# First attention of a two-layer network on one Trainium2 core: the maxima enter the scores as two more rows of the turned queries

## The reference

```python
    def _L0_attn_ref(...):
        scale = 1.0 / np.sqrt(D)
        sin, cos = _rope_tables(n, D)
        qkv = (x @ w_qkv.T + b_qkv).reshape(b, n, 3, H, D).transpose(2, 0, 3, 1, 4)
        q, k, v = (qkv[0], qkv[1], qkv[2])
        q = jax.nn.elu(q) + 1.0
        k = jax.nn.elu(k) + 1.0
        q = _apply_rope(q, sin, cos)
        k = _apply_rope(k, sin, cos)
        attn = jnp.einsum('bhnd,bhmd->bhnm', q, k) * scale
        attn = jax.nn.softmax(attn, axis=-1)
        attn_out = jnp.einsum('bhnm,bhmd->bhnd', attn, v)
        ...
        return attn_out + lepe
```

## Time and profile before

| | us |
|---|---|
| median of 3 runs | 1029.71 |
| lowest, highest of the 3 | 1021.74, 1030.68 |
| the profiled execution | 1020.3 |
| its span in the trace | 1018.5 |
| PE busy over the span | 862.1 (85%) |
| DVE busy over the span | 749.3 (74%) |
| mean granted TensorE clock | 0.915 |

### The profile page before, as it was taken

One profiled execution on the slowest core, in us unless ns is written; L12 is line 12 of the kernel. 1 busy time (PEld: TensorE's weight loads), 2 busy tenths in 40 slices (PEclk: granted clock), 3 DMA queues, 4 the chain that ended last, 5 costly groups with the idle time before them and its releaser, 6 DMA issues.

```text
span 1018.5 us, 23321 instructions
## 1 busy us (share of the span) xinstructions
PE 862.1 (85%) x7492; PEld 655.8 (64%) x7492; DVE 749.3 (74%) x2654; ACT 520.8 (51%) x1365; POOL 284.5 (28%) x395
## 2 busy tenths in 40 slices
PE   4899989999996899945999188999999998548992
PEld 3457856667765457833999166677767776437992
DVE  7758888788767866877577658877787778566675
ACT  4233044666564223014465238877887788434653
POOL 3034035634001003117755180001000000077741
PEclk9999995999996999965899679999999999859996
DMA  9204079810006304056231256645454552343313
GB/s 238 71 1 141 1 280 374 264 52 2 2 1 161 80 1 141 1 168 187 80 84 34 84 147 194 185 123 159 149 174 139 157 155 84 92 143 90 104 36 125
DMA packets 134947, 119.74 MB, mean 118 GB/s; under 512 B 10755, under 2 KB 115227, under 8 KB 134836
## 3 DMA queue, kind: packets, MB, share of 16 engines
q1 hardware_dynamic: 130292, 109.83, 36.4%
q0 software_dynamic: 4544, 8.54, 2.5%
HBM read 67.45 MB, written 51.80 MB: 117 GB/s over the span
## 4 chain that ended last, share of the span: by engine, by line
PE 63%; DVE 16%; ACT 12%; issue 4%; DMA 3%; DVEq 1%; SPq 0%; POOL 0%; POOLq 0%; ACTq 0%
PE psum L955 7%; PE psum L964 6%; PE psum L1551 6%; PE psum L1465 5%; ACT a_L L2799 3%; ACT a_L L2797 3%; PE psum L2139 3%; PE psum L2669 3%; PE psum L2718 3%; PE psum L2077 3%; PE psum L2705 2%; PE psum L2042 2%; PE psum L743 2%; PE psum L1491 2%; ACT a_PT L2808 2%
## 5 line engine op out<-in xcount | busy, mean ns | idle before, releaser
L2297 DVE TENSOR_REDUCE a_negmax<-psum 128x2 f32<-128x512 f32 x128 | 83.7, 684 | 20.9 <-PE psum L2077 19.5
L2246 ACT ACTIVATE a_PT<-psum 128x1024 f32<-128x1024 f32 x64 | 65.5, 1023 | 26.2 <-PE psum L2122 25.8
L2799 ACT ACTIVATE a_L<-a_L,a_least 128x256 f32<-128x256 f32 x128 | 63.3, 495 | 0.0
L1010 ACT ACTIVATE f_hT<-psum,f_wt 128x128 f32<-128x128 f32 x156 | 44.5, 369 | 36.5 <-PE psum L955 36.5
L1010 ACT ACTIVATE g_hT<-psum,g_wt 128x128 f32<-128x128 f32 x156 | 44.4, 370 | 33.3 <-PE psum L955 33.3
L2669 PE MATMUL psum<-a_KT,a_Q 64*128 64x128 f32 (+1 forms) x512 | 57.6, 342 | 3.3 <-DVE a_least L2859 0.9
L2797 ACT ACTIVATE a_L<-a_L,a_least 128x128 f32<-128x128 f32 x128 | 50.6, 395 | 10.7 <-DVE a_least L2859 9.8
L2857 DVE CUSTOM_DVE_ANT_0 a_L<-psum,a_X 128x128 f32<-128x128 f32 x128 | 36.6, 286 | 25.0 <-PE psum L2669 24.9
L2116 PE MATMUL psum<-a_turned 24*128 24x256 f32 x256 | 53.8, 359 | 0.0
L2859 DVE CUSTOM_DVE_ANT_0 a_L<-psum,a_X 128x256 f32<-128x256 f32 x128 | 53.7, 420 | 0.0
L2808 ACT ACTIVATE a_PT<-psum 128x768 f32<-128x768 f32 x64 | 51.2, 800 | 1.7 <-PE psum L2685 0.9
(11 more groups left out here) (579 smaller groups left out, 2563.3 us busy)
## 6 DMA issues: line engine op xcount, KB each, us to landing
z<-a_G SPq DMA_DIRECT2D x32, 512.0 KB, 3.5
a_X<-z SPq DMA_DIRECT2D x16, 1024.0 KB, 6.7
f_slots_dram<-empty SPq DMA_DIRECT2D x1, 8910.0 KB, 28.1
g_slots_dram<-empty SPq DMA_DIRECT2D x1, 8910.0 KB, 51.6
a_X<-z SPq DMA_DIRECT2D x16, 512.0 KB, 4.1
f_wgu<-in_gate_up SPq DMA_DIRECT2D x16, 384.0 KB, 6.6
z<-pad SPq DMA_DIRECT2D x6, 1024.0 KB, 9.7
g_wgu<-in_gate_up SPq DMA_DIRECT2D x16, 384.0 KB, 6.5
```

The source lines that it names most:

```text
L1010: act.activation(hT[:, i % 2, c, :], bank[i % 2][:, P * c:P * c + P], ACT.Relu, bias=wt[i % WBUF][:, B1 + c:B1 + c + 1]).then_inc(relu_don ...
L2246: act.activation(PT[m % 4][:, :, :, :].rearrange("p j t n -> p j (t n)"), core.psum[:, 2 + 2 * (u % 2):4 + 2 * (u % 2), :], ACT.Exp, scale ...
L2297: dve.tensor_reduce(negmax[:, :, h], query_bank(b, h).rearrange("p (t n) -> p t n", n=SEQ), AX.X, ALU.max, negate=True).then_inc(max_done, 1)
L2799: act.activation(pr[:, o, P:3 * P], L[:, o, P:3 * P], ACT.Exp, bias=least[:, o, 1:2], scale=-1.0, accum_out=sums[:, o, 1:2]).then_inc(p_re ...
```

## The change

`select` and the bfloat16 matmuls that used it are gone. The two parts of the negated maxima are written by DMA into rows 24 and 25 of each head's band in the turned queries (`SHIFTED` = 26), and the same two rows of the turned keys hold 1.0, which GpSimd writes into `stack` before it is turned. So one matmul on 26 rows gives the shifted scores. `shift` now has 32 partitions of float32, and a0's `sync` issues eight transfers for each sequence (4 partitions of 256 floats each) as soon as `shift` is ready; by key waits for `rows_written`.

SP's program has `fills.sync` and `write_pads` ahead of a0's `sync` now.

From n = 0 on, by query of the odd head is woven into by key (`scores`), by query of the even head follows it, and one VectorE instruction (`two_maxima`) takes the maxima of both heads from banks 0 and 1. The first matmul into bank 1 waits until the maxima of the step before are taken from both banks, and so does the first into bank 0.

`turn_maxima` and `take_shift` stand at u = 5 and `values_and_convolution` at u = 6.

```diff
...
-    mparts = sb("mparts", [P, 2, 4, 2 * H0], BF16)
-    shift = [sb(f"shift{i}", [P, SEQ], BF16) for i in range(2)]
+    mparts = sb("mparts", [P, 2, 2 * H0])
+    shift = [sb(f"shift{i}", [2 * H0, SEQ]) for i in range(2)]
...
+
+        for b in range(BATCH):
+            sp.wait_ge(shift_ready, b + 1)
+            for part in range(2):
+                for g in range(GROUPS):
+                    s = H0 * part + HG * g
+                    sp.dma_start(turned[b % NT][0][PARTS + part::HW, g, :],
+                                 shift[b % 2][s:s + HG, :]).then_inc(rows_written, 16)
+
+    WRITES = 2 * GROUPS * 16
...
         for m in stack:
-            pool.memset(m[:, :, :, :, PARTS:HW].rearrange("p a t h d -> p (a t h) d"), 0.0).then_inc(filled, 1)
+            pool.memset(m[:, 0, :, :, PARTS:HW].rearrange("p t h d -> p (t h) d"), 0.0).then_inc(filled, 1)
+            pool.memset(m[:, 1, :, :, PARTS:SHIFTED].rearrange("p t h d -> p (t h) d"), 1.0).then_inc(filled, 1)
+            pool.memset(m[:, 1, :, :, SHIFTED:HW].rearrange("p t h d -> p (t h) d"), 0.0).then_inc(filled, 1)
...
-        def scores_by_query(b, h):
-            n, g, rows = b * H0 + h, h // HG, slice(HW * (h % HG), HW * (h % HG) + PARTS)
-            if h % (2 * HG) == 0:
+        def place_for_query(b, h, order):
+            if h % (2 * HG) in (0, 1):
                 pe.wait_ge(tk_ready, 4 * b + 2 * (h // (2 * HG)) + 2)
-            if n >= 2:
-                pe.wait_ge(max_done, n - 1)
+            if order >= 2:
+                pe.wait_ge(max_done, min(order - 1, H0 * b + h - h % 2))
+
+        def by_query(b, h, t):
+            g, rows = h // HG, slice(HW * (h % HG), HW * (h % HG) + PARTS)
             q, k = turned[b % NT]
+            last = pe.matmul(bank[h % 2][:, SEQ * t:SEQ * t + SEQ], q[rows, g, P * t:P * t + P].bitcast(F32R),
+                             k[rows, g, :].bitcast(F32R), start=True, stop=True)
+            if t:
+                last.then_inc(s1_done, 1)
+
+        def by_key(b, u, j, t):
+            h = 2 * u + j
+            g, rows = h // HG, slice(HW * (h % HG), HW * (h % HG) + SHIFTED)
+            q, k = turned[b % NT]
+            return pe.matmul(bank[2 + 2 * (u % 2) + j][:, SEQ * t:SEQ * t + SEQ], k[rows, g, P * t:P * t + P].bitcast(F32R),
+                             q[rows, g, :].bitcast(F32R), start=True, stop=True)
+
+        def scores_by_query(b, h, order):
+            place_for_query(b, h, order)
             for t in range(2):
-                last = pe.matmul(bank[h % 2][:, SEQ * t:SEQ * t + SEQ], q[rows, g, P * t:P * t + P].bitcast(F32R),
-                                 k[rows, g, :].bitcast(F32R), start=True, stop=True)
-            last.then_inc(s1_done, 1)
+                by_query(b, h, t)
...
             for t in range(2):
-                last = pe.transpose(bank[T].bitcast(BF16)[:, P * t:P * t + P],
-                                    mparts[:, t, :, :].rearrange("p i h -> p (i h)"), core.identb[:, :])
+                last = pe.transpose(bank[T][0:2 * H0, P * t:P * t + P], mparts[:, t, :], core.ident[:, :])
...
-        def scores_by_key(b, u):
+        def scores(b, u, second):
             m = b * STEPS + u
+            if second:
+                place_for_query(*second, second_order(*second))
+                by_query(*second, 0)
             if u == 0:
-                pe.wait_ge(shift_ready, b + 1)
+                pe.wait_ge(rows_written, WRITES * (b + 1))
             if m >= 2:
                 pe.wait_ge(p_ready, m - 1)
-            q, k = turned[b % NT]
             for t in range(2):
+                if second and t:
+                    by_query(*second, 1)
                 for j in range(2):
-                    h = 2 * u + j
-                    rows = slice(HW * (h % HG), HW * (h % HG) + PARTS)
-                    pe.matmul(bank[2 + 2 * (u % 2) + j][:, SEQ * t:SEQ * t + SEQ],
-                              k[rows, h // HG, P * t:P * t + P].bitcast(F32R), q[rows, h // HG, :].bitcast(F32R),
-                              start=True, stop=False, skip_group_check=True)
-                for j in range(2):
-                    h = 2 * u + j
-                    rows = slice(HW * (h % HG), HW * (h % HG) + HW)
-                    last = pe.matmul(bank[2 + 2 * (u % 2) + j][:, SEQ * t:SEQ * t + SEQ], select[rows, h, :],
-                                     shift[b % 2][rows, :], start=False, stop=True, skip_group_check=True)
+                    last = by_key(b, u, j, t)
             last.then_inc(s2_done, 1)
...
                 if n == 0:
-                    pe.wait_ge(max_done, H0 + 4)
-                scores_by_key(i, u)
+                    pe.wait_ge(max_done, H0 + 6)
+                scores(i, u, due[1])
...
-            if u == 6 and inside(i + 1):
+            if u == 5 and inside(i + 1):
                 turn_maxima(i + 1)
...
-            if due[1] and n not in PAIRED:
-                scores_by_query(*due[1])
+            if due[1] and n < PAIRED.start:
+                scores_by_query(*due[1], H0 * due[1][0] + due[1][1])
...
+        def two_maxima(b, h):
+            dve.wait_ge(s1_done, H0 * b + h + 2)
+            if h == 0:
+                dve.wait_ge(parts_ready, b)
+            dve.tensor_reduce(negmax[:, :, h:h + 2].rearrange("p t j -> p j t"),
+                              core.psum[:, 0:2, :].rearrange("p j (t n) -> p j t n", n=SEQ), AX.X, ALU.max,
+                              negate=True).then_inc(max_done, 2)
...
         def take_shift(b):
             dve.wait_ge(parts_turned, b + 1)
             if b >= 2:
-                dve.wait_ge(s2_done, STEPS * (b - 1))
-            dve.tensor_copy(shift[b % 2][:, :], bank[T].bitcast(BF16)[:, 0:SEQ]).then_inc(shift_ready, 1)
+                dve.wait_ge(rows_written, WRITES * (b - 1))
+            dve.tensor_copy(shift[b % 2][:, :].bitcast(F32R), bank[T][0:2 * H0, 0:SEQ]).then_inc(shift_ready, 1)
...
-            if u == 7 and inside(i + 1):
-                take_shift(i + 1)
-            if due[0]:
-                maximum(*due[0])
+            if due[0] and n < 0:
+                maximum(*due[0], H0 * due[0][0] + due[0][1])
+            elif due[0]:
+                two_maxima(*due[0])
...
-            if due[1]:
-                maximum(*due[1])
+            if due[1] and n < 0:
+                maximum(*due[1], H0 * due[1][0] + due[1][1])
+            if u == 5 and inside(i + 1):
+                take_shift(i + 1)
...
             for n, st in enumerate(made):
-                st["sync"](sp)
                 if names[n] == "a0":
                     fills.sync(sp)
                     core.early.write_pads(sp)
+                st["sync"](sp)
```

44 lines of the change are left out of this document (20 added, 24 removed).

## The result

The changed kernel takes 1084.06 us (median of 4 executions, 1082.61 to 1085.97), the kernel before 1028.61 us beside it (4 executions, 1021.74 to 1030.68). The ratio is 1.056, 95% interval 1.0512 to 1.0608: slower by 55 us. The profiled execution took 1085.2 us, its span is 1083.5.

What follows compares the result with a forecast made beforehand. TensorE was taken to bound a0, with SP's queue causing the new wait. 1020.3 + 50 (initial wait) + 1 (steady steps) + 3 (row writes) = 1074.3, plus half of 9.4 to the median: 1079 us; range 1060 to 1100, own range 1068 to 1092.

Steps and rivals of the forecast that it cites:

- The initial wait: Start of a0: sequence 0's row writes stand behind the pads in SP's queue, so by key goes on 50 us late.
- The issue: SP's eight row writes of a sequence: 0.47 us each with the gap, the eighth starting 3.3 us behind the first.
- The row writes of sequences 1 to 7: Later sequences in a0: TensorE waits briefly for their rows, 3 us in sum, bounds 1 and 23.
- The two-bank maximum: VectorE's one maximum over 1024 columns in a0: 1.23 us, bounds 1.1 and 1.38.
- The block: TensorE's eight float32r matmuls of a step in a0: 0.75 us, bounds 0.46 and 0.92.
- The hand-overs: Delays in a0's even steps: VectorE starts 0.04 us after the matmul, TensorE wakes 0.05 us after the maximum.
- the loop: Steps with by query: TensorE and VectorE's two-bank maximum wait for each other, 2.14 us a round, no such step shorter.
- The steady steps: All eight sequences of a0, without row waits: changes in step times sum to +1.0 us, bounds -21 and +17.
- The clock: Rival: TensorE idles in even steps and its clock falls; 15 us a sequence, 1109 us for two; chance 0.08.
- a clock of 0.50 in the steady part: Listed sign that the forecast is wrong: TensorE's clock at 0.50 in a0's steady part.
- The cold restart: Steps 0 to 3 after the wait run cold as before: nothing, up to 5 us if the cold stretch gets longer.
- The offset to the median: Half of the 9.4 us by which the profiled execution of before lies below its median, added to the sum.

Runs made afterwards that it cites:

- The repeat: The kernel before, unchanged, profiled once more: 1029.58 us, with its first attention stage a0 at 191.5 us instead of 180.6.

## Why the prediction was right, and where it was not

Forecast 1079, measured 1084.06, in the range of 1060 to 1100 and in the forecast's own range. The mechanism of the large term was right; that the number came so close is in part luck, as the end of this section shows.

1. *The initial wait, 50 us.* By key came 48.9 us later. The reason given is right for 45 of them, in which TensorE stood idle for the rows. The step "Its preparation, up to n = -1, is as before and ends at about 163.9 us" was wrong: it ended at 167.76, for the waits shown above, and took 4 us out of the wait. SP began the rows at 207.13 instead of 208.8, since the pads took 17.32 us to issue instead of 18.11 and began 1.3 earlier, while the wait for them was 0.4 longer. Two runs show the cause: moving the rows in SP's queue moved the start by the same amount, and giving them to ScalarE's queue, in two transfers, moved it by 42 us and brought some 47 of the 55 back.
2. *The issue.* Eight took 4.5 us (207.13 to 211.65), 0.57 each with its gap, where the term had 0.47. From the first issue to by key it was 5.7 us, where 5.2 stood.
3. *The row writes of sequences 1 to 7, +3.* Within its bounds: TensorE waited 1.7 us for them. In these sequences the eight small writes, against which the prediction held the rule of the Trainium skill, DMA: Bandwidth & Descriptors, section "Rules for kernel authors", on coalescing, cost no more than that.
4. *The two-bank maximum, 1.23.* Right: 1224 ns is the mean of 53.

```profile
L2326 DVE TENSOR_REDUCE a_negmax<-psum 128x4 f32<-128x1024 f32 x53 | 64.9, 1224 | 74.9 <-PE psum L2093 72.8
```

5. *The block, 0.75.* Wrong: 0.45, its lower bound. I read the old block as showing no overlap beyond two; the new order has heads of four bands behind one another, and the three rows from 271.64 on have the first five of the eight begun or queued within 0.02 us of one another.
6. *The hand-overs, 0.04 and 0.05.* Too small: 0.17 and 0.15. Errors 5 and 6 cancel, and the loop came out at 2.07 where 2.14 stood.
7. *The steady steps, +1 in all, at an unchanged clock.* This step failed. Against the same lucky profile of before, the pace cost 18.8 us where steps and row waits had 4; against the usual one, 8. The piece that was missing is the clock. The sum was made from pieces at 1.00 (`values` in 1.07 us), while after runs its first 34 us from by key on and a part of each sequence at 0.50, where the same sixteen matmuls take 1.93:

```profile
284.04 0.35 PE L2093 MATMUL psum<-a_turned 24*128 24x256 f32 x1 [1.14 <-DVE a_negmax L2326]
...
285.01 1.93 PE L2162 MATMUL psum<-a_PT,a_Vs 128*32 128x256 f32 x16 [0.38 <-DVE a_attn L2365]
```

   The prediction had this as a rival ("The clock", 0.08), priced at 15 us a sequence and 30 for two. It was true as a mechanism and took another form: a short fall in each sequence, and not two whole sequences. One of the prediction's own signs of being wrong, a clock of 0.50 in the steady part, was there from 346 to 362 us, and the stage ended 68 us later instead of 54. The one test of the size is the pair of runs with and without filled gaps, 8.6 us over seven sequences, or about 1 us each; it is a test beside a kernel whose start was filled as well, and against after only 4.0 us, not clear of the noise. So how much of the slower pace is the clock and how much the loop itself stays open; undoing the two-bank instruction takes the loop and the gaps away together (5.1 us of waiting for maxima instead of 20.0). The clock should have been a part of the forecast and not a rival of 0.08. The Trainium skill, TensorE: Matmul & The Clock Gate, section "A second HAM failure mode: psum-queue depth-cycling", had described small idle times between groups that move the clock in another kernel. The windows agree with it; the first is before, with 19.24 of 20 us at work, the second after, with 17.08 and the clock at 0.91 on average:

```profile
226.00:246.00 20.00, 19.24 (x211) 13.86 (x209) 16.16 (x38) 11.97 (x16) 6.99 (x10) 1.00 0.01 2
```

```profile
283.00:303.00 20.00, 17.08 (x176) 10.92 (x176) 15.36 (x30) 11.36 (x16) 7.01 (x10) 0.91 0.01 3
```

8. *The cold restart counted as nothing, up to 5 us if the stretch gets longer.* It got longer: 34 us from by key on, where before had some 12 (to 176 us). Sequence 0 took 26.1 us against 20.8 and 22.3 in the two profiles of before, 4 to 5 us more, with the clock at 0.50 throughout; only sequence 6 differs by as much. The kernel with matmuls in the wait was no faster, but its clock fell again at once, so it does not show that the cold costs nothing.
9. *The offset to the median, +4.7.* Half of it was added for want of a cause. The repeat shows the cause, a clock that fell in one profile of before and not in the other. With what was measured, the sum is 1020.3 + 48.9 + 18.8 - 3 = 1085.0, after's profiled time within 0.2; this is an account of two profiles and no test. Of the 18.8, 11 are the better execution of before that it is compared with (149.0 against 160.0 us from first by key to the end).

So the forecast was right by its large term, the place in SP's queue, and wrong in the pace. From its 1079 to the measured median: the pace +14.8, the wait -1.1, the other stages -3, the offset -4.7, and -1.1 since after's profiled execution lies that much above its median; the sum is 1083.9. The pace alone would have moved the forecast to 1094. That it ended 5 us off is luck: the half offset and the shorter stages behind a0, which have nothing to do with the mechanism, and two small terms took 10 of those 15 us back.

## What to carry to other kernels

Before a transfer is put on a queue, list what stands ahead of it there at that moment, pads and fills that nobody waits for included. Where a list must be early in part and late in part, no place in one engine's queue is right. Here another engine's queue, with fewer and larger transfers, was worth some 47 us.

Look for what moved ahead of a wait as well. The steps before the first by key had been taken as unchanged, and by key was ready 4 us later.

When one instruction takes the place of two, look at what it releases. Two reads of 0.69 us gave one bank back early; one read of 1.23 us gives both back late and turns an overlap into a loop: less work for VectorE, and the kernel 6 us longer.

Where work is taken from the engine that bounds a stage, look at its clock again: here TensorE went from 19.24 to 17.08 of 20 us at work, and the clock from 1.00 to 0.91. Take a second profile of the kernel before as well: two executions of it differed by 11 us in one stage (180.6 and 191.5), and of the twelve further executions beside it ten took 1027.5 us or more, like the longer one.

## What the runs showed of the hardware that was not expected

- Float32r matmuls on 24 or 26 rows in four different bands ran side by side: eight of 256 columns in 0.45 us, where each by itself is listed with 0.28 to 0.48.
- TensorE's clock stayed at 0.50 from 212.8 to about 247 us although TensorE was 9.23 and 8.94 of 10 us under way at that level; in before it fell after two windows with 3.02 and 3.08 of 4 us of work, and not after one with 3.31. In before with one more matmul a step it fell at 168 us with 3.85 of 4 us at work. I have no rule that fits all of these.
- Matmuls whose results are thrown away, put into the gaps of the steps, made a kernel 8.6 us faster (ratio 1.0494 against 1.059). Put into a wait of 45 us alone they gained nothing: the clock was at 1.00 at 212 us and at 0.50 by 220.
- A transfer of 4 KB within on-chip memory kept SP for 0.57 us with its gap; the same data in 16 KB pieces cost ScalarE 1.10 us for two, with 2.5 us of idle time in front of the next exponential:

```profile
210.19 1.10 ACTq L1956 DMA_DIRECT2D a_turned<-a_shift  x2
211.39 1.02 ACT L2268 ACTIVATE a_PT<-psum 128x1024 f32<-128x1024 f32 x1 [2.52 <-issue]
```
